# Two buffers for the last block's bf16 tokens, and a new written-out order for all engines, in a four-block transformer kernel

## The reference, cut to what matters

```python
x = L0_attn_x                                   # 256 channels
xn = _layernorm(x, axis=-1)
x = x + _L0_attn_ref(xn, ...) + _L0_ffn_ref(xn, ...)   # 16 heads; ternary weights
xn = _layernorm(x, axis=-1)
x = x + _L1_attn_ref(xn, ...) + _L1_ffn_ref(xn, ...)   # gated scan; 16 experts, top 2
xn = _layernorm(x, axis=-1)
x = x + _L2_attn_ref(xn, ...) + _L2_ffn_ref(xn, ...)   # one head; weights made by splines
xn = _layernorm(x, axis=-1)
x = x + _L3_attn_ref(xn, ...) + _L3_ffn_ref(xn, ...)   # 16 x 16 heads, rotary; 8 experts in bf16, top 2
return x
```

```python
xb = flat.astype(jnp.bfloat16)
ge = jnp.einsum('nh,eih->nei', xb, wg)
ue = jnp.einsum('nh,eih->nei', xb, wu)
he = jax.nn.sigmoid(ge) * ue
de = jnp.einsum('nei,ehi->neh', he, wd)
routed = (comb.astype(jnp.bfloat16)[:, :, None] * de).astype(jnp.float32).sum(axis=1)
```

## Time and profile before

| what | value |
|---|---|
| median of three runs | 1230.7 us (1230.67 to 1230.82) |
| span of the profiled execution | 1229.5 us |
| PE busy | 1096.5 us (89%) |
| DVE busy | 864.2 us (70%) |
| ACT busy | 631.2 us (51%) |
| POOL busy | 503.0 us (41%) |
| mean granted clock of PE | 0.951 |

### The profile page before, as it was taken

One profiled execution on the slowest core, in us unless ns is written; L12 is line 12 of the kernel. 1 busy time (PEld: TensorE's weight loads), 2 busy tenths in 40 slices (PEclk: granted clock), 3 DMA queues, 4 the chain that ended last, 5 costly groups with the idle time before them and its releaser, 6 DMA issues.

```text
span 1229.5 us, 17428 instructions
## 1 busy us (share of the span) xinstructions
PE 1096.5 (89%) x6541; PEld 718.4 (58%) x6556; DVE 864.2 (70%) x1612; ACT 631.2 (51%) x963; POOL 503.0 (41%) x551
## 2 busy tenths in 40 slices
PE   4579999999999998999389999998789998996998
PEld 2356686765665564675268898987234543553445
DVE  6988767678658999856667326368776779668751
ACT  4445656475568875643235224252176276455473
POOL 5655748466514544413764214053331321141131
PEclk9769999999999999999689999999699999998999
DMA  5905335443260000267350000008626316317220
GB/s 178 291 10 156 81 96 161 126 123 107 49 207 35 35 35 9 82 206 243 94 52 26 1 1 1 1 26 201 156 51 155 108 45 165 92 49 173 71 72 18
DMA packets 86115, 116.42 MB, mean 95 GB/s; under 512 B 29616, under 2 KB 43280, under 8 KB 85264
## 3 DMA queue, kind: packets, MB, share of 16 engines
q1 hardware_dynamic: 47792, 70.28, 19.1%
q0 software_dynamic: 38240, 45.03, 14.7%
HBM read 81.54 MB, written 40.40 MB: 99 GB/s over the span
## 4 chain that ended last, share of the span: by engine, by line
PE 64%; DVE 21%; ACT 5%; issue 4%; POOL 3%; DMA 2%; another core or an unknown queue 0%; SPq 0%; ACTq 0%; DVEq 0%; POOLq 0%
PE pair L691 22%; PE bank L691 19%; PE bank L770 7%; PE pair L760 5%; PE pair L749 5%; DVE max L1152 4%; ACT probs L1670 2%; POOL gathered L2082 1%; PE pair L710 1%; PE bank L778 1%; DVE hidden L1208 1%; DVE hidden L1206 1%; DVE tern_mask L1049 1%; PE pair L790 1%; DVE mix_h L1540 1%
## 5 line engine op out<-in xcount | busy, mean ns | idle before, releaser
L1152 DVE TENSOR_REDUCE max<-pair 128x2 f32<-128x1024 f32 (+3 forms) x256 | 252.6, 1020 | 64.1 <-PE pair L749 36.6
L1670 ACT ACTIVATE probs<-pair 128x1024 f32<-128x1024 f32 (+3 forms) x256 | 213.4, 865 | 112.9 <-PE pair L760 106.4
L749 PE MATMUL pair<-ks,qs 64*128 64x512 f32 (+3 forms) x512 | 111.7, 457 | 28.7 <-DVE max L1152 13.9
L770 PE MATMUL bank<-probs,v 128*32 128x512 f32 (+3 forms) x1024 | 119.0, 542 | 2.0 <-ACT probs L1670 1.3
L760 PE MATMUL pair<-qs,ks 64*128 64x512 f32 (+3 forms) x512 | 103.8, 437 | 13.7 <-DVE max L1152 4.9
L2003 POOL TENSOR_TENSOR h_low<-hidden,h_high 128x512 fp32r<-128x512 f32 x64 | 83.3, 1307 | 77.4 <-ACT h_high L1708 77.0
L749 PEld LDWEIGHTS pair<-ks,qs 64*128 64x128 f32 x512 | 50.8, 198 | 89.2 <-DVE max L1152 35.1
L760 PEld LDWEIGHTS pair<-qs,ks 64*128 64x128 f32 x512 | 46.5, 190 | 81.2 <-ACT probs L1670 25.9
L2100 POOL TENSOR_TENSOR h<-mix_h,h 128x512 bf16<-128x512 f32 x48 | 54.8, 1169 | 75.4 <-DMA h<-comb 49.7
L1702 ACT ACTIVATE hidden<-pair 128x512 f32<-128x512 f32 x64 | 38.0, 597 | 86.5 <-PE pair L691 72.6
L2047 POOL TENSOR_SCALAR_AFFINE_SELECT probs<-probs 128x256 f32<-128x256 f32 x128 | 51.3, 411 | 65.0 <-ACT probs L1670 63.8
(11 more groups left out here) (327 smaller groups left out, 2678.5 us busy)
## 6 DMA issues: line engine op xcount, KB each, us to landing
kept<-q_high SPq DMA_DIRECT2D x64, 256.0 KB, 3.7
qs<-kept POOLq DMA_DIRECT2D x32, 512.0 KB, 4.2
ks<-kept POOLq DMA_DIRECT2D x32, 512.0 KB, 5.2
kept<-q_low SPq DMA_DIRECT2D x32, 256.0 KB, 4.1
expert_in<-in_experts_in SPq DMA_DIRECT2D x16, 352.0 KB, 4.3
expert_out<-in_experts_out SPq DMA_DIRECT2D x16, 256.0 KB, 5.5
h<-comb SPq DMA_DIRECT2D x4, 1024.0 KB, 5.4
x<-in_x SPq DMA_DIRECT2D x4, 512.0 KB, 5.1
```

Of the source, the lines that this page charges most:

```text
L749: made = mm(to[:, hh, 0:n], m.qs[k][slot][r0:r0 + STACK, p, qt * P:(qt + 1) * P], m.ks[k][slot][r0:r0 + STACK, p, 0:n], start=True, stop=k ...
L770: made = mm(to[32 * j:32 * j + 32, q0:T], m.v[b % 2][:, kt, G * g + j, :], m.probs[(2 * kt + j // 2) % 4][:, j % 2, q0:T], start=kt == 0, ...
L1152: V.tensor_reduce(m.max[:, g % 2, :, p, qt], to[:, :, 0:n], AX.X, ALU.max).then_inc(*s.done("top"))
L1670: A.activation(m.probs[(2 * kt + p) % 4][:, :, q0:T], to[:, :, q0:T], ACT.Exp, scale=0.25).then_inc(*s.done("exp"))
```

## The change

The buffer x16 becomes two, and batch b uses number b % 2. The votes (the router's logits), which lay behind it, move to another place. turned(3,b) waits for the mixes of batch b - 2 instead of b - 1. The tables DUE and TAKEN are written anew for all engines: by the tables 467 of PE's 1098 parts change their place in its order, 465 of DVE's 844, 529 of ACT's 857, 290 of POOL's 429 and 34 of SP's 165, most of them by 1 to 10 places. Among them: turn(3,0) goes from 664 to 646 on PE, comb_turn(0) from 676 to 682, behind score(3,0,1,0,0); on POOL cast3 goes ahead of bring(3,0,1), and spline_low(2,1) ahead of gather(0,0).

```diff
-        self.x16 = sb("x16", 100, [P, KC, T], BF16)
+        self.x16 = [sb(f"x16_{i}", 100 + 2 * i, [P, KC, T], BF16) for i in range(2)]
...
-        self.h16, self.votes = sb("h16", 190.125, [P, MIX, T], BF16), sb("votes", 102, [P, 2, TT, E3])
+        self.h16, self.votes = sb("h16", 190.125, [P, MIX, T], BF16), sb("votes", 204.25, [P, 2, TT, E3])
...
-            made = products(to[:, part, :], [(m.w16_in[:, kc, c0:c0 + P], m.x16[:, kc, :]) for kc in range(KC)])
+            made = products(to[:, part, :], [(m.w16_in[:, kc, c0:c0 + P], m.x16[b % 2][:, kc, :]) for kc in range(KC)])
...
-                dve.wait_ge(*at("probs_turn", BATCH - 1, 1))
+                dve.wait_ge(*at("probs_turn", BATCH - 1, 3))
...
-            if b > 0:
-                act.wait_ge(*s.last("mix", [(b - 1, j) for j in range(MIX)]))
+            if b >= 2:
+                act.wait_ge(*s.last("mix", [(b - 2, j) for j in range(MIX)]))
             else:
-                act.wait_ge(*at("probs_turn", BATCH - 1, 0))
-            A.copy(m.x16[:, :, :], to[:, :, :]).then_inc(*s.done("turned"))
+                act.wait_ge(*at("probs_turn", BATCH - 1, b))
+            A.copy(m.x16[b % 2][:, :, :], to[:, :, :]).then_inc(*s.done("turned"))
```

Of the table DUE, some of the shorter lines (turns of PE, then of POOL):

```diff
-    "turn": "1 52 144 207 375 432 444 469 582 598 623 646 664 711 829 952",
+    "turn": "2 52 141 207 374 433 444 469 582 598 624 645 646 711 829 952",
-    "comb_turn": "676 780 874 981",
+    "comb_turn": "682 784 877 985",
-    "bring": "12 13 18 45 65 76 92 118 133 148 161 175 189 200 212 222 345 346 349 363 368 370 371 384 388 390 392 394 408 410 412 413",
+    "bring": "12 14 17 48 65 76 90 120 136 148 159 176 188 200 212 224 345 347 348 364 369 370 371 385 388 390 392 394 406 408 412 414",
-    "gather": "283 285 286 287 289 290 293 292",
+    "gather": "284 285 286 287 289 290 291 294",
-    "spline_low": "276 277 280 279 278 281 282 284 296 294 295 298",
+    "spline_low": "276 277 279 278 280 282 281 283 292 297 296 295",
-    "cast3": "347",
+    "cast3": "346",
```

More of the change, by code:

```diff
@@ L319 @@
 TAKEN = {name: [int(bank) for bank in banks] for name, banks in {
-    "tern_sum": "040400240442",
-    "turn": "2224040202422044",
-    "qk": "4224402002024242",
-    "vals": "2004224404004244",
-    "score": "4424000404044040404022244200222420024404024240044042004402404442402020444424400020040244024400024442202004400020204020220044424004020424022244442440440240420044424420200424020402024004020002022004042204020242242200024424200242202404044224042400202200420420",
-    "prob": "2220042002044000204242442202024020242024424204420002200424202224242420240242202040222400020224240442044042040202242024040240424022424402244220422200220204240242042022420040244044044440024404404204224004402020002422420204024024022004240442404424024442000420",
@@ L326 @@
-    "weigh": "77776666666666666666666677776666666677777777777766666666666666667777666666666666777766667777666677776666777777777777777777776666",
-    "back": "77677667666677777776767676766677",
-    "rows": "402004020442",
-    "out": "76677767666776767676766776667667",
-    "unit": "2402020420004202220202044042044220422040024204202044200424402044",
-    "down": "77767677",
-    "mean": "6777",
-    "proj": "0044022402200440",
-    "gate": "7766667776676776",
-    "gamma": "4024",
-    "inflow_turn": "0202",
@@ L337 @@
-    "mem_turn": "77777677",
-    "shared": "0202440220420402",
+    "tern_sum": "240400240442",
+    "turn": "2242004222242044",
+    "qk": "4224202400024242",
+    "vals": "2002200224004242",
+    "score": "2424000400424020404022242420022424020204024240042042004424444000402024004224400020040044024420024442202040040420004024424024422004020424022240442440420240420040020424000424240402224404020202024004042204020242002422044422202240222402044224040024202200420400",
+    "prob": "2440402002042400042442442402024020422042244024420022400424402224242420240242202040022400020244244402020442044002242420424020424042424402244224422200224204220424002002400040244044044440024402404204220204402020004442420204044024022004224240424422024402400420",
@@ new lines @@
+    "weigh": "77776666666677777777666677776666777766666666666677776666666666666666777766666666777777776666666677776666777766667777777777776666",
+    "back": "66777677777777767777677776766776",
+    "rows": "202004020442",
+    "out": "66766677767676766766776767666676",
+    "unit": "2402020420004240440204244042244240422040202404242044204000404044",
+    "down": "77766677",
+    "mean": "6776",
+    "proj": "0004224002204040",
+    "gate": "7776777767666776",
+    "gamma": "0024",
+    "inflow_turn": "2202",
@@ L339 @@
+    "mem_turn": "66777667",
+    "shared": "2204440220420402",
     "count": "6666",
     "logit_turn": "7777",
-    "merge": "76",
-    "expert_turn": "6676777777676666",
-    "expert_in": "4240020424400204",
-    "expert_fold": "7667766667777666",
-    "expert_out": "6667766667767767",
-    "spline": "204024242042",
-    "qk2": "4420",
-    "v2": "76766767",
-    "score2": "6776676766677676",
-    "probs_turn": "7676677667767776",
-    "comb_turn": "6767",
-    "mix": "402042020240040402024220200402424220422402004224",
+    "merge": "67",
@@ L353 @@
+    "expert_turn": "6767776777766666",
+    "expert_in": "4240044404020244",
+    "expert_fold": "7667767676766766",
+    "expert_out": "6667666776767767",
+    "spline": "024024000240",
+    "qk2": "2204",
+    "v2": "67766767",
+    "score2": "6677677766777667",
+    "probs_turn": "7676676666677676",
+    "comb_turn": "7767",
+    "mix": "402042020240240402024222200402424220402402004224",
 }.items()}
```

## The result

The changed kernel takes 1250.1 us (median of four runs, 1247.4 to 1254.3), the kernel before in the same comparison 1230.8. The ratio is 1.0158, 95% interval 1.013 to 1.0186: slower by 19 us, where 1237.0 was forecast and 1241 was the upper end of the range. The profiled execution spans 1246.1 us, 16.6 more than before.

The account below looks back on a forecast made before the run. No single bound: the chain of waits is 64% PE, 21% DVE. Terms 5.8 - 1.0 + 1.0 + 0.5 = +6.3, and 1229.5 + 6.3 + 1.2 = 1237.0 us; 8-in-10 range 1226.5 to 1241.

Parts of the forecast that it names:

- The two buffers: bf16 token copy and votes: the copy finds its buffer free anyway, PE's own order covers the wait; priced at 0.
- The cast ahead of bring(3,0,1): Start of block 3: queue q0 serves in order, so the bring lands about 868 us and the tops end later; +5.8 us.
- a sign of being right: Trace after: w_in issued about 850.5 us, PE waits 5 to 8 us for ks, SP's comb store about 15 us later.
- The upper bound of +8.8: Cast step in block 3: if the cast shares the engines with more than now, the bring lands at 871 us.
- comb_turn's new place: PE, start of block 3: later comb store and load hidden, 0; up to +3 if comb's load comes after the first mix.
- All local exchanges of neighbours: Blocks 1 and 3: each a few places beside a full engine; 0, with +-2 as bound, together with the first 64 us.
- turn(3,0) early and two pairs: Last units of block 2 have two PSUM pairs instead of three, just enough; +0.5 us, bounds 0 and +3.
- The gathers: 585 to 655 us: gathers begin +1.5 us later, 2.5 us of DVE's idle time goes; -1.0 us, bounds -5.5 and +4.8.
- PSUM repeats: Consecutive users taking the same PSUM pair, 16 times before and 37 after, 12 new in block 0; +1.0 us, bounds 0 and +4.
- C: Rival: larger stall plus late comb, two pairs too few and PE pauses in block 0; 1240 to 1243 us, chance 0.15.

Follow-up runs that it names:

- buffers_only: The kernel before with the two token buffers, the votes' new place and their waits, order and PSUM places left as before: ratio 0.9971.
- before_cast: The kernel before with one part moved, cast3 ahead of bring(3,0,1) on POOL: ratio 1.0137, 1247.4 us against 1228.9.
- both_back: The changed kernel with cast3 behind bring(3,0,1) again, and rope(0,1) behind q_low(3,0,0) with q_high put back: ratio 1.0098, 1243.1 us.
- units_only: The kernel before with the new order and places only from turn(2,3) to block 2's last units, turn(3,0) early, two pairs: ratio 1.0021.
- early_only: The kernel before with the changed kernel's order and places only up to block 2's third batch: ratio 1.0021.
- window_only: The kernel before with the new order and places only between block 2's third batch and block 3's first mixes: ratio 1.0113, 1244.5 us.
- places: The kernel before with other PSUM pairs for block 3's first sixteen scores and DVE's tops in PE's order: ratio 0.9985.
- cast_comb: The kernel before with cast3 ahead of bring(3,0,1) and comb_turn(0) behind score(3,0,1,0,0): ratio 1.0083.
- last_only: The kernel before with the changed kernel's order and places only from qk(3,3,0) on: ratio 1.0076.

## Why the prediction was wrong

**The two buffers at 0.** Right as far as the profile goes: the copy stands 2.03 us behind its turn as before, and B of buffers_only is within 0.4 us. Whether its ratio of 0.9971 is more than scatter is open.

**The cast ahead of bring(3,0,1), +5.8 us.** The mechanism was right: the order of landing, and a wait of 7.45 us at the forecast score. The size was not: the last top came 14.7 us later. The term is a chain of times, and each link can be read from the traces (us; before_cast shifted by the 2.8 us by which it reaches turn(2,3) earlier):

| | forecast | changed kernel | before_cast |
|---|---|---|---|
| bring(3,0,0) is there | 852.5 | 862.7 | 855.6 |
| the cast has landed | 865 | 873.5 | 867.8 |
| bring(3,0,1) is there | 868 | 876.2 | 875.9 |
| the last of the sixteen tops ends | 883.2 | 892.2 | 894.5 |

In the changed kernel the cast and the bring behind it took no longer than forecast: 13.5 us from the one bring to the other against 15.5, and the second bring came 2.7 us behind w_out, as at 0.34 MB/us. What failed is the start. w_in was issued at 856.61 us, where about 850.5 had been named as a sign of being right, SP's store of comb went out 24.6 us later than before, where about 15 had been named, and the first bring was there 10.2 us later than the sum had it. About 3 of these are a misreading of the kernel before: in before_cast, where nothing ahead of the first bring is moved, it is there at 855.6, not 852.5. The other 7 come from exchanges that were priced at 0 or nearly so (below). That the wait itself fell inside the forecast 5 to 8 us is luck: both of its ends moved by 8.

In before_cast the start is nearly right, and the move by itself costs 17.0 us in B for another reason. The bring behind the cast was costed at 0.34 MB/us, a rate read where the queue q1 was idle; it ran at 0.12 beside SP's load of comb and took 8.0 us instead of 3.1. The upper bound of +8.8 left too little for that. In the changed kernel comb_turn's new place keeps that load away, which is worth 5.9 us in B; I had priced it at 0 and only as a danger.

The tops were counted wrong too. PE makes four scores ahead of the wait in the new order, as the sum has it, but on DVE the top of score(3,0,1,0,0) stands fourth, so three tops are ahead of the wait and thirteen behind it, where the sum has four and twelve: 1.1 us too little. Of the one pause of 1 us that the sum kept 0.2 is left, so the last top ends 15.9 us behind the arrival of the bring, where the sum has 15.2.

The rule of the Trainium skill (DMA: Bandwidth & Descriptors, section Queues, rings and completion order) that descriptors of one ring are taken in order stands with the four landings above. That engines go round between rings by packets fits too, better than I said: beside the cast q0 and q1 moved 59 and 40 packets, and q1 had 5.1% of the engines' time since those of q0 held 12 KB each; beside the bring they moved 306 and 425, those of q0 held 1.9 KB, and q1 had 74.5%.

**All local exchanges of neighbours, 0 with +-2.** This is the step that failed outright: it moved the start of the cast by most of 7 us, and it made the whole loss of C. Among them was rope(0,1) ahead of q_low(3,0,0), 4.1 us by itself, and split_high(2) ahead of q_high(3,0,1), which starts POOL's two operations under rope(0,1); in both_back, where q_low's place is mended, these and the units leave 4.0 us, of which the units' part is 2.2, although the pauses of the tops are gone there too. Further on, the exchanges of block 3's later batches cost 4.4 to 5.1. "A few places beside a full engine" was the wrong question: DVE was not full there, and the overtaken part was what SP's stores, and then a bring, waited for.

**turn(3,0) early and two pairs, +0.5 (0 to 3).** Inside its bounds, 2.2 measured, the upper part of them. Two pairs are not just enough: PE waits 1.59 us for a pair in units_only and 1.58 in the changed kernel, where before it did not wait.

**The gathers, -1.0.** Not decided. The first gather goes out 1.7 us later (586.36 us), near the 1.5 taken. DVE's idle time of 4.21 us is gone as hoped, but the one ahead of the row of line 1096 that follows the gathers grew from 3.68 to 6.75 us. From turn(1,3) to turn(2,1), where the gathers lie, the kernels take 207.8 to 218.7 us with the order of before and 210.9 to 221.4 with the new one, so a gain of 1 us can't be seen. **PSUM repeats, +1.0.** Not tested by themselves. early_only, which holds most of the new ones, has a ratio of 1.0021 with an interval that holds 1; by the tables, nine of the new repeats lie between turn(0,3) and turn(1,2), where some 2 us are lost, but these may be theirs or the new order's.

**How the parts add.** In B the cast takes 17.0, comb_turn gives 5.9 back, q_low's place takes 4.1, the units 2.2: 17.4, where the window takes 12.9 (window_only) and 13.8 (after). What is missing in that list is the new PSUM places and order of the tops: without the three pauses the last top ends 15.9 us behind the arrival of the second bring in the changed kernel, where it takes 18.6 in before_cast; places, which changes only that, gives 3.9 back. With it the list comes to 13.5. The times of arrival bear this out. From cast_comb to the changed kernel the first bring comes 7.2 us later and the second 7.3 (counted from turn(2,3)), so a first bring that is late is not hidden under the second wait, it moves it. But the fit is no proof that the parts are independent: with the cast back, B is still 7.1 above before, where 4.1, 2.2 and -3.9 make 2.4. Which other parts of the window make up the difference, a later comb among them, was not tested. Of the rivals, C named the right kind (a larger stall and two pairs too few), but 1243 was still 7 us short.

**Open.** What costs the 3 us ahead of turn(3,3) in last_only, what the new order loses between turn(0,3) and turn(1,2), and why C of before_cast is 338.0, have no run of their own.

## What to carry to other kernels

In an order written by hand, an exchange of two neighbours is not priced by how far they move or by how full their engine is, but by what the overtaken part releases: follow it through stores, queue and load to the first instruction that waits for it. On a DMA queue that is served in order, put a large transfer behind all small ones that are needed sooner, even when it is itself needed soon; and price a transfer that is pushed back at the rate it gets beside whatever else has been pushed back with it. Don't check a forecast by the length of a wait alone, since both of its ends can move together: compare the arrival of each transfer, counted from a row that all kernels have. And put back all parts of a window, then one at a time, with the parts that win among them.

## What the runs showed of the hardware that was not expected

A casting transfer takes nearly all of the DMA engines' time from another queue (97.5% against 5.1% in before_cast) while it moves only 0.2 MB/us (0.72 MB in 3.6 us), where plain transfers of the same queue moved 0.34. The other queue had work all that time: the keeps that SP issued from 851.6 us on took some 13 us to land, where one issued from 844 to 850 us took 4.8.

A DVE operation with two operands in SBUF that comes while POOL already runs an operation on SBUF takes longer: line 1111 2.69 us instead of 1.23, line 1113 2.74 instead of 0.69. In the kernel before, line 1111 took 3.31 us in rope(0,0), beside POOL's line 1991. The Trainium skill (SBUF — State Buffer, section SBUF: two separate sides) says that these two engines share one pair of ports, and that the one that comes second waits until the other is done; the traces agree, as each of the long operations spans an end of a POOL operation. In the changed kernel the second of POOL's two, which starts while line 1111 is still at work, takes 3.34 us where it took 2.39 before.
